# The first GAT layer of a graph network in column groups, its self-loop products moved to ScalarE

## What is computed

```python
h = (x @ W).reshape(N, H, C)
logits = leaky_relu(alpha_s[src] + alpha_d[dst], 0.2)
m = segment_max(logits, dst)
e = exp(logits - m[dst])
s = segment_sum(e, dst)
out = segment_sum(h[src] * (e / s[dst])[:, :, None], dst) + b
```

## Time and profile before

| | |
|---|---|
| runs (3) | 4652.38, 4662.45, 4663.33 us; median 4662.45 |
| the profiled execution | 4651.74 us, its span 4649.9 us |
| granted TensorE clock, mean | 0.533 |
| busy | VectorE 2475.6, POOL 2782.0, PE 1426.0, ScalarE 960.7 us |
| DMA | 398.82 MB, mean 86 GB/s |

### The profile page before, as it was taken

The page is one execution under the profiler, slowest core; times in us unless marked ns, Lnnn a source line. Parts: engine busy times, 40 slices in busy tenths (PEclk is TensorE's granted clock), DMA queues, the critical chain, the costliest instruction groups (busy, mean ns, idle before and its releaser), DMA issues. The chain is left out here.

```text
span 4649.9 us, 35089 instructions
## 1 busy us (share of the span) xinstructions
PE 1426.0 (31%) x5413; PEld 1238.2 (27%) x5413; DVE 2475.6 (53%) x5048; ACT 960.7 (21%) x2420; POOL 2782.0 (60%) x2525
## 2 busy tenths in 40 slices
PE   2888177771040002653400000000000057245121
PEld 2888066661030001542300000000000045134121
DVE  4556066660687848762078853334864423353454
ACT  1555044440020000210100011221000024123110
POOL 7777777777206750027750047777248877777687
PEclk9555555555555555655555555555555556556555
DMA  3666155541011100324403345554001145344011
GB/s 82 184 190 194 43 135 138 138 132 37 7 47 37 28 14 23 90 68 104 128 4 91 97 118 146 146 149 135 6 10 19 18 115 157 103 113 131 16 17 17
DMA packets 258339, 398.82 MB, mean 86 GB/s; under 512 B 91231, under 2 KB 95209, under 8 KB 258241
## 3 DMA queue, kind: packets, MB, share of 16 engines
q1 hardware_dynamic: 171022, 322.96, 23.0%
q0 software_dynamic: 87264, 75.37, 9.8%
HBM read 186.08 MB, written 213.11 MB: 86 GB/s over the span
## 5 line engine op out<-in xcount | busy, mean ns | idle before, releaser
L806 PE MATMUL banks<-ident,cross_in 125*2 125x125 f32 (+3 forms) x26 | 10.5, 405 | 1993.8 <-DVE cross_in L829 1341.9
L593 PE MATMUL banks<-node_w,x_t 65*125 65x200 f32 x1600 | 551.9, 537 | 0.0
L806 PEld LDWEIGHTS banks<-ident,cross_in 125*2 125x2 f32 (+3 forms) x26 | 3.0, 116 | 1998.4 <-DVE cross_in L829 1345.0
L593 PEld LDWEIGHTS banks<-node_w,x_t 65*125 65x125 f32 x1600 | 515.8, 330 | 3.4
L215 POOL DMA_INDIRECT edge_rows<-x_rows,src_i x400 | 402.1, 1005 | 129.1 <-issue 129.1
L273 POOL DMA_INDIRECT x_rows<-r_x,src_scat_i x200 | 257.3, 1287 | 122.0 <-issue 122.0
L273 POOL DMA_INDIRECT norm_rows<-edge_rows,scat_i x200 | 257.7, 1288 | 74.2 <-issue 74.2
L273 POOL DMA_INDIRECT out_dram<-n_out,scat_i x200 | 250.9, 1254 | 78.5 <-issue 60.6
L636 DVE TENSOR_REDUCE n_var<-n_sq 125x8 f32<-125x512 f32 x125 | 85.6, 686 | 317.7 <-ACT n_sq L650 317.6
L215 POOL DMA_INDIRECT edge_rows<-x_rows,norm_s x200 | 207.7, 1039 | 64.1 <-issue 64.1
L215 POOL DMA_INDIRECT edge_rows<-in_x_dram,src_i x200 | 205.1, 1025 | 67.7 <-issue 63.7
(11 more groups left out here) (346 smaller groups left out, 5036.7 us busy)
## 6 DMA issues: line engine op xcount, KB each, us to landing
h_rows<-r_h SPq DMA_DIRECT2D x125, 462.0 KB
x_rows<-r_x SPq DMA_DIRECT2D x125, 241.5 KB
x_rows<-r_x SPq DMA_DIRECT2D x125, 224.0 KB
r_x<-x_rows SPq DMA_DIRECT2D x125, 224.0 KB
x_rows<-n_out SPq DMA_DIRECT2D x125, 224.0 KB
n_in<-in_x_dram SPq DMA_DIRECT2D x100, 224.0 KB
n_c<-x_rows SPq DMA_DIRECT2D x100, 224.0 KB
out_dram<-n_out SPq DMA_DIRECT2D x100, 224.0 KB
```

The source lines that it names most:

```text
L593: done = pe.matmul(product[h][:, n // 2, n % 2, :], x_t[u][:, at:at + P], node_w[:, :], start=True, stop=True)
L806: pe.transpose(bank[0][0:cols, 0:rows], frm, ident[0:rows, 0:rows]).then_inc(s_tout, 1)
```

## The change

- The edge columns of the first GAT layer are worked in groups of 10, 8, 4 and 3 chunks. POOL gathers with a semaphore per group (`s_got`). `running_softmax` keeps a running maximum (`peaks`) and mass (`masses`), and rescales the running sums at each column with a factor from ScalarE (`scales`). The 128 scans of a group start from the last column of the group before. `merge_own` merges in the self-loop; its factors lie in `mixes`.
- POOL no longer takes part in the weighting; VectorE weights chunk by chunk.
- ScalarE forms the self-loop products of a chunk, 16 activations of 125x64 with a pointer scale (`own_chunk`), one chunk ahead, straight into `e_dup`. VectorE multiplies the two sums with their factors, waits for `own` and adds.
- Carries are dealt with at the end: every mixed row also goes to a new DRAM tensor ED. After the last group `ends_in` works out what comes in over the partition's edge; POOL gathers from ED one row per partition (the end of its first run), VectorE corrects it, it goes through PE and ScalarE once more, and POOL scatters it to `h2_rows`. `first_ends`, in the first block, finds these rows.
- The own logits (with their hold) stand ahead of the sort instead of behind it. Crossings of this block use PSUM bank 7.
- `sum_rows_dve`, in the other four blocks too, waits after every second scan (`SCANS_BETWEEN`).
- `GROUPS` loses its boundary at 24, for the cosine block too. The three float copies of the keys go; the comparisons read the integer planes. The sort's turns use the semaphores of the crossings.

```diff
-GROUPS = (0, 10, 18, 22, 24, 25)
+GROUPS = (0, 10, 18, 22, 25)
...
+SCANS_BETWEEN = 2
...
     for f in range(D):
         done = dve.tensor_tensor_scan(rows[:, :, f], cont[:, :], rows[:, :, f], 0.0, ALU.mult, ALU.add)
-    v.link(done)
+        if f % SCANS_BETWEEN == SCANS_BETWEEN - 1:
+            v.link(done)
...
+def first_ends(dve, place, tmp, at):
+    v.link(dve.tensor_tensor(first_end[:, :], reach_f[:, :], last[:, :], ALU.mult))
+    v.link(dve.tensor_tensor(tmp, first_end[:, :], place, ALU.mult))
+    dve.tensor_reduce(at[:, 0:1], tmp, AX, ALU.add)
...
+    v.link(dve.tensor_scalar(pass_pen[:, :], reach_f[:, J - 1:J], 1.0, -LOW, ALU.subtract, ALU.mult))
...
+        first_ends(dve, heads[1][:, :], heads[0][:, :], carry_in)
...
+def own_logits(dve):
...
+    for h in range(H):
+        v.link(dve.scalar_tensor_tensor(selfs[h][:, :], selfs[h][:, :], 0.2, selfs[h][:, :], ALU.mult, ALU.max))
+    over_segments(dve, "hold", [d[:, :] for d in dens])
+    v.link(dve.memset(peaks[:, :, 0:1], LOW))
...
+def running_softmax(dve, s, rows, at, n, sums, weigh):
+    a, b = (NC * c for c in groups[n])
+    c = slice(a, b)
+    for h in range(H):
+        done = dve.tensor_tensor(scales[:, 2 + h, c], rows[:, c, at + h], dens[h][:, c], ALU.add)
+    v.link(done)
+    for h in range(H):
+        done = dve.scalar_tensor_tensor(scales[:, 2 + h, c], scales[:, 2 + h, c], 0.2, scales[:, 2 + h, c], ALU.mult, ALU.max)
+    v.link(done)
+    for h in range(H):
+        done = dve.tensor_tensor_scan(peaks[:, h, a + 1:b + 1], pen_f[:, c], scales[:, 2 + h, c], peaks[:, h, a:a + 1], ALU.add, ALU.max)
+    v.link(done)
+    for h in range(H):
+        dve.tensor_tensor(scales[:, 2 + h, c], scales[:, 2 + h, c], peaks[:, h, a + 1:b + 1], ALU.subtract)
+        done = dve.tensor_tensor(scales[:, h, c], peaks[:, h, a:b], peaks[:, h, a + 1:b + 1], ALU.subtract)
+    v.link(done)
+    for h in range(H):
+        done = dve.scalar_tensor_tensor(scales[:, h, c], scales[:, h, c], 0.0, pen_f[:, c], ALU.min, ALU.add)
+    done.then_inc(s.args, 1)
+    dve.wait_ge(s.exps, 2 * n + 1)
+    for h in range(H):
+        done = dve.tensor_tensor_scan(masses[:, h, c], scales[:, h, c], scales[:, 2 + h, c], masses[:, h, a - 1:a] if a else 0.0, ALU.mult, ALU.add)
+    v.link(done)
+    for i in range(*groups[n]):
+        v.link(weigh(dve, slice(i * NC, i * NC + NC)))
+    for h in range(H):
+        for f in range(D):
+            done = dve.tensor_tensor_scan(sums[h][:, c, f], scales[:, h, c], sums[h][:, c, f], sums[h][:, a - 1, f:f + 1] if a else 0.0, ALU.mult, ALU.add)
+            if f % SCANS_BETWEEN == SCANS_BETWEEN - 1:
+                v.link(done)
...
+def merge_own(dve, s, n, share):
+    a, b = (NC * c for c in groups[n])
+    c, w = slice(a, b), slice(0, b - a)
...
+        dve.tensor_tensor(mixes[:, h, w], peaks[:, h, a + 1:b + 1], scales[:, 2 + h, c], ALU.subtract)
+        done = dve.tensor_tensor(mixes[:, 2 + h, w], selfs[h][:, c], scales[:, 2 + h, c], ALU.subtract)
+    done.then_inc(s.args, 1)
+    dve.wait_ge(s.exps, 2 * n + 2)
...
+    for k in range(2 * H):
+        done = dve.scalar_tensor_tensor(mixes[:, k, w], mixes[:, k, w], share, scales[:, 2 + k % H, c], ALU.mult, ALU.mult)
+    done.then_inc(s.args, 1)
...
+def ends_in(dve, s, sums):
+    first_at(dve, lambda h: selfs[h][:, :], first_peak)
+    first_at(dve, lambda h: scales[:, h, :], first_mass)
+    carry_dve(dve, peaks[:, :, J], H, "max", peak_in)
+    v.link(dve.scalar_tensor_tensor(peak_all, peak_in, pass_pen[:, :], peaks[:, :, J], ALU.add, ALU.max))
...
+    for h in range(H):
+        transpose_dve(dve, dve.tensor_copy(cross_in[0:P, 0:D + 1], end_exp[:, h:h + 1].to_broadcast([P, D + 1])))
+        dve.tensor_copy(pass_scaled[0:D + 1, :], crossings["bank"][0:D + 1, 0:P])
+        v.link(dve.memset(crossed[0:D + 1, 0:1], 0.0))
+        dve.tensor_scalar(cross_in[0:P, 0:D], sums[h][:, J - 1, :], end_exp[:, 2 + h:3 + h], None, ALU.mult)
+        transpose_dve(dve, dve.tensor_scalar(cross_in[0:P, D:D + 1], masses[:, h, J - 1:J], end_exp[:, 2 + h:3 + h], None, ALU.mult))
+        transpose_dve(dve, dve.tensor_tensor_scan(crossed[0:D + 1, 1:P + 1], pass_scaled[0:D + 1, :], crossings["bank"][0:D + 1, 0:P], 0.0, ALU.mult, ALU.add))
+        dve.tensor_copy(mass_in[:, h:h + 1], crossings["bank"][0:P, D:D + 1])
+        v.link(dve.tensor_copy(carry_rows[h][:, :], crossings["bank"][0:P, 0:D]))
...
+        tail_xa.fetch(g)
+        for n, (start, end) in enumerate(groups):
+            cols = range(start * NC, end * NC)
+            gather(g, xa, X1, src_place_i, s_got[n], cols[0:TAIL_STEPS[0]])
+            if n == 0:
+                tail_xa.put_down(g)
+            gather(g, xa, X1, src_place_i, s_got[n], cols[TAIL_STEPS[0]:])
+            if n == 0:
+                tail_xa.place(g, s_first)
+        for u in range(U):
+            g.wait_ge(s1.mixed[u], ROWS_DONE * ((ECH + 1 - u) // 2))
+        g.wait_ge(s1.turned, ECH)
+        g.indirect_dma_start(out=first_mixed.rearrange("p h f -> p (h f)"), out_offset=None, in_=ED,
+                             in_offset=bass.IndirectOffsetOnAxis(ap=first_i[:, :], axis=0)).then_inc(s_first, 16)
+        for u in range(U):
+            g.wait_ge(s1.stored[u], ROWS_DONE * ((ECH + 1 - u) // 2))
+        g.wait_ge(s1.row, ECH + 1)
+        g.indirect_dma_start(out=H2, out_offset=bass.IndirectOffsetOnAxis(ap=first_scat_i[:, :], axis=0), in_=first_row, in_offset=None,
+                             bounds_check=last_row(g, ROWS), oob_is_err=False).then_inc(s_first, 16)
+        g.wait_ge(s_first, 48)
...
         sort_fill_dve(dve)
+        own_logits(dve)
         sort_start_dve(dve)
         sort_dve(dve, PARTS[0], held[0], held[1])
-        attention_dve(dve, s1, xa, D + 1)
-        v.link(weigh1(dve, v, VECTOR_COLS))
...
+        def weigh(dve, c):
+            v.link(dve.tensor_tensor(vb[:, c, :], xa[:, c, 0:D], wide(scales[:, 3, c]), ALU.mult))
+            return dve.tensor_tensor(xa[:, c, 0:D], xa[:, c, 0:D], wide(scales[:, 2, c]), ALU.mult)
+        dve.wait_ge(s_first, 16)
+        for n, (start, end) in enumerate(groups):
+            dve.wait_ge(s_got[n], got_done(n, 1))
+            running_softmax(dve, s1, xa, D + 1, n, sums, weigh)
+            merge_own(dve, s1, n, 1.0)
+            for i in range(start, end):
+                u, c, w = i % 2, slice(i * NC, i * NC + NC), slice((i - start) * NC, (i - start) * NC + NC)
+                parts = (n_sq[u], n_in[u])
+                for h in range(H):
+                    done = dve.tensor_tensor(parts[h][:, :, :], sums[h][:, c, :], wide(mixes[:, h, w]), ALU.mult)
+                v.link(done)
+                dve.wait_ge(s1.own, i + 1)
+                for h in range(H):
+                    done = dve.tensor_tensor(e_dup[u][:, :, h, :], e_dup[u][:, :, h, :], parts[h][:, :, :], ALU.add)
+                done.then_inc(s1.x, 1)
+        ends_in(dve, s1, sums)
+        dve.wait_ge(s_first, 32)
         for h in range(H):
-            sum_rows_dve(dve, sums[h], carry_rows[h])
...
+        def turn_chunk(i):
+            u = i % 2
+            pe.wait_ge(s1.x, i + 1)
+            if i >= 2:
+                pe.wait_ge(s1.turned_sb, i - 1)
...
+        def heads_chunk(i):
+            u = i % 2
+            pe.wait_ge(s1.turned_sb, i + 1)
+            if i:
+                pe.wait_ge(s1.row, i)
...
+        for start, end in groups:
+            for i in range(start, end):
+                turn_chunk(i)
+                if i > start:
+                    heads_chunk(i - 1)
+            heads_chunk(end - 1)
+        ends_pe(pe)
...
+        def own_chunk(i, start):
+            u = i % 2
+            act.wait_ge(s1.loaded[u], ROWS_DONE * (i // 2 + 1))
+            if i >= 2:
+                act.wait_ge(s1.turned, i - 1)
+                act.wait_ge(s1.mixed[u], ROWS_DONE * (i // 2))
+            for c in range(NC):
+                w = (i - start) * NC + c
+                for h in range(H):
+                    done = nc.scalar.activation(e_dup[u][:, c, h, :], r_x1[u][:, c, 0:D], ACT.Copy, scale=mixes[:, 2 + h, w:w + 1])
+            done.then_inc(s1.own, 1)
...
+        for n, (start, end) in enumerate(groups):
+            logits_act(act, s1, n)
+            if n:
+                turned_chunk(start - 1)
+                row_chunk(start - 2)
+                row_chunk(start - 1)
+            merged_act(act, s1, n)
+            act.wait_ge(s1.args, 3 * n + 3)
+            own_chunk(start, start)
+            for i in range(start, end - 1):
+                own_chunk(i + 1, start)
+                turned_chunk(i)
+                if i > start:
+                    row_chunk(i - 1)
+        turned_chunk(ECH - 1)
+        row_chunk(ECH - 2)
+        row_chunk(ECH - 1)
+        ends_act(act, s1)
...
+        for i in range(ECH):
+            u = i % 2
+            sp.wait_ge(s1.x, i + 1)
```

(44 more changed lines are left out.)

240 lines of the change are left out of this document (129 added, 111 removed).

## The result

The changed kernel takes 4703.27 us (median of 3 runs, 4697.02 to 4706.58) against 4662.45 before: ratio 1.0092, 95% interval 1.0065 to 1.0119. It is slower by some 41 us; 4700 was forecast. The profiled execution took 4697.02 us, its span is 4695.2 (before 4649.9), so between the two traces there are 45.3 us to account for.

The account below looks back on a forecast made before the run. VectorE's own work and the chunk pipeline were taken to bound the first GAT block: 1626.3 + 201.5 + 230 + 26.5 = 2084.3 us, +26; with +12 elsewhere, 4662 + 38 = 4700 us, range 4645 to 4738.

Parts of the forecast that it names:

- The start: First GAT block: VectorE's row work begins at 1626.3 us, right behind the sort; the 59 us gather wait is gone.
- (e): First GAT block: the overlap fails and VectorE waits for gathers, marked by a wait on edge rows; excluded, no chance given.
- Scan phases: First GAT block, four groups: 512 scans 138 us, weighting 36, short operations and exponentials 27; together 201.5 us.
- Rival (b): Waits between scans cost nothing, in the first GAT stage and elsewhere: 42 us fall away, 4658 us; chance 0.05.
- Chunk phases: First GAT block: transfers and ScalarE's products run one after the other, 12.5 us a chunk, 230 us in all.
- (c): Chunk loop: transfer chain longer, 9 us a cycle because mixed stores write more; +36 us, 4736 us; chance 0.10.
- (d): Several sizes partly better: pointers at half price, transfers 5.5 us a cycle; 4664 us, 4650 to 4675; chance 0.13.
- The tail: End of the first GAT block, after the last sum: crossings, last mixed store, gather, correction and scatter, 26.5 us.
- Other stages: Outside the first GAT block: scan waits +10.5 us on gate, second GAT and cosine rows, set-up +2; +12 in all.
- first-ends work: First block: nine short operations, about 2.4 us, less 0.65 for three copies that go: +2 us.
- The sum: Whole kernel: +26 us in the first GAT block and +12 elsewhere, +38 on the 4662 us median, gives 4700 us.

Follow-up runs that it names:

- the mended kernel: Changed kernel without waits between scans and with SyncE's row store behind the next mixed store and load: 4578.38 us against 4647.18 for the kernel before, ratio 0.9863.

## Why the prediction was right

**The start.** 1626.3 was forecast, 1628.83 came. Of the 2.5 us the earlier stages add 1.9 (VectorE's first instruction of the block stands at 1414.68 instead of 1412.76); the own logits fit into the wait, and no wait for edge rows is left, so (e) was rightly excluded.

**Scan phases.** 201.5 forecast, 204.7 measured (60.3, 59.9, 44.2, 40.3). The rates are 0.290, 0.316, 0.252 and 0.237 us a scan against 0.29, 0.31, 0.25 and 0.23. The two parts of the fixed cost were measured alone: the wait 0.139 (0.12 taken from the sort's rows), the pointer 0.060 (0.06 taken). Rival (b) is false: 248 waits between narrow scans cost 34.4 us. The Trainium skill, "VectorE: DVE Perf Modes", The DRAIN you can't avoid, finds that a semaphore after each operation costs nothing extra, for eight copies in a row; for the scans here the measurement decides otherwise.

**Chunk phases.** 230 forecast, 232.8 measured (105.3, 81.4, 30.7, 15.4 against 105, 80, 30, 15). The cycle is 12.5 us, as its four parts made it: wait 6.35 (6.2), products 3.92 (3.85), copies as said. The run with another order of SyncE's shows that the named cause, transfers issued behind the row copies and ScalarE standing in order before them, makes 80 us. (c) did not come about: the wait is 6.35 us and not 9. Nor did (d): the pointers cost their full price and the transfers were no quicker.

**The tail** is the term that was mis-sized: 26.5 forecast, 33.9 measured. The working gave the crossings their own time on PE, 7.2 us, and put at nothing what is queued ahead of them there: the heads products of two chunks, for which VectorE waits 8.20 us. In the mended kernel it is still 10.1 us, so a better order of PE's last instructions is the next thing to try; it wasn't tried.

**Other stages.** +12 forecast; +1.9 came ahead of the block and +3.9 behind it. The new first-ends work makes VectorE's part of the set-up 1.3 us longer, but the node pass behind it starts only 0.1 later (80.88 instead of 80.77), because VectorE waits there for its input anyway: this term was 0, not 2. The rows of 64 scans got longer by more than the 3.5 each: 3.9 (gate), 4.5 (second GAT), 3.9 (cosine), 4.2 (message). But the second GAT block as a whole got only 2.1 us longer, the cosine block 1.2 and the message block 0.6; the gate block got 5.4 longer, after it had started 3.5 earlier. What gives these microseconds back was not looked for.

**The sum.** The block itself makes 39.5 us instead of 26, the other stages 5.8 instead of 12. Between the traces that is 45.3 against 38. The two errors, 13.5 up and 6 down, partly cancel, and against the medians, 41 against 38, only 3 are left. That closeness is partly luck: the interval of the first measurement reaches from 30 to 56 us, and the second gave +60. What the runs bear out is the mechanism and the size of its two main terms.

## What to carry to other kernels

Write down, for each transfer in a pipelined loop, what its queue waits for just ahead of it: a store that depends on the end of the chunk, issued ahead of the next load, turns double buffers into a chain, and moving it behind that load gave 80 us here. A wait between narrow independent instructions costs the overlap of the two on top of the idle time that the profile prints (6.4 us beside 2.1 in 128 scans here); where they are independent, one wait behind a whole row of them is enough. A gain that consists in a wait removed is worth what the race behind that wait leaves, and the other side of the race (here the sort) may run differently on another chip.

## What was not expected of the hardware

On two of the chips the kernel before takes some 1,780 us more, and the changed one 1,830. In their traces VectorE works through the sort at 60.58 us busy in 274 while POOL issues its 211 gathers, and at 114.56 in 148 behind them (the windows above); on the first chip it is busy 177 of 200 us beside 155 gathers. The missing time stands before VectorE's instructions in the sort as waits of up to 4.7 us that no semaphore of the program explains, and in the node pass as such waits of up to 66 us. POOL's gathers in the sort's time are no slower there (0.986 us each against 0.995). What holds the engines up is open. It changes the cost of this change from +41 or +60 to +111 us, and leaves the 471 to 474 us behind the gathers as they are.

PE's granted clock rose with SyncE's new order: in the first group's chunks it is 0.53 in the changed kernel and in the one without scan waits, nearly always at the lower level (0.50, 1.2 GHz), but 0.73 in the one with the new order and 0.68 in the one with both, partly at the upper; PE is busy 62 of 105 us in the changed kernel and 49 of 65 in the one with both. The heads products and the turn of a chunk take 7.6 us at the lower level (1705.33 to 1712.9 in the mended kernel's timeline) and fit no cycle of 6.2, so the mended loop partly lives on the upper one. With the new order alone ten cycles lie below 7.6 us and take 66.4 us together; at 7.6 each they would take 9 or 10 us more. So, as an estimate, that much of the 80 us is the clock's and the rest the order's; no run held the clock at one level.
